# A fused mixture-of-experts layer with fp32 split products: up sum and h of both tiles in PSUM, and a new order of products and copies

## The reference

```python
g = jnp.einsum('bsd,edf->ebsf', h, Wg)
u = jnp.einsum('bsd,edf->ebsf', h, Wu)
expert_outs = jnp.einsum('ebsf,efd->ebsd', jax.nn.silu(g) * u, Wd)
expert_output = jnp.einsum('be,ebsd->bsd', gating_probs, expert_outs)
shared = jnp.einsum('bsf,fd->bsd', jax.nn.silu(h @ Sg) * (h @ Su), Sd)
out = x + (1.0 - sg) * expert_output + sg * shared
```

## Time and profile before

| what | value |
|---|---|
| median of 3 runs | 2305.16 us (2304.65 to 2307.76) |
| profiled execution | 2306.76 us |
| its span, first to last instruction | 2305.0 us |
| mean granted TensorE clock | 0.998 of full speed |
| TensorE busy | 2246.9 us (97%), 9504 matmuls |
| DVE, POOL, ACT busy | 78%, 72%, 62% |
| HBM traffic | 53 GB/s over the span |

### The profile page before, as it was taken

How to read it: one execution, slowest core, us unless ns; L and a number is a source line. 1 busy time by engine, 2 the same in 40 slices (tenths; PEclk the granted TensorE clock), 3 DMA queues, 4 the chain that set the end, 5 groups by cost and what they waited for, 6 DMA issues and landing times.

```text
span 2305.0 us, 33781 instructions
## 1 busy us (share of the span) xinstructions
PE 2246.9 (97%) x9504; PEld 1765.6 (77%) x9504; DVE 1802.1 (78%) x2622; ACT 1430.8 (62%) x2334; POOL 1651.5 (72%) x2055
## 2 busy tenths in 40 slices
PE   6999999999999999999999999999999999999998
PEld 4777777777777777777777777777777777777776
DVE  6777777777777777777777777777778778777787
ACT  5666666666666666666666666666666666666664
POOL 7877777777887767767787677677676677677663
PEclk9999999999999999999999999999999999999999
DMA  4111111111111111111121111111112111111110
GB/s 136 55 48 55 48 48 55 48 48 55 60 56 48 52 51 48 51 51 48 50 64 56 48 48 55 48 48 55 48 48 67 55 48 48 54 48 49 54 48 25
DMA packets 44170, 122.21 MB, mean 53 GB/s; under 512 B 4928, under 2 KB 4944, under 8 KB 44128
## 3 DMA queue, kind: packets, MB, share of 16 engines
q1 hardware_dynamic: 44064, 121.65, 17.1%
q0 software_dynamic: 64, 0.07, 0.1%
HBM read 117.51 MB, written 4.19 MB: 53 GB/s over the span
## 4 chain that ended last, share of the span: by engine, by line
PE 49%; DVE 25%; issue 16%; ACT 8%; DVEq 1%; ACTq 1%; DMA 0%; SPq 0%; POOL 0%
DVE h L422 16%; PE chain_ps L256 9%; DVE up L450 8%; ACT tap_p L353 7%; PE chain_ps L258 6%; PE down_ps L256 6%; PE down_ps L258 6%; PE chain_ps L257 6%; PE down_ps L257 6%; PE p_ps L256 3%; PE p_ps L257 3%; PE p_ps L258 3%; DVEq L118 0%; ACTq L118 0%; DMA acc<-xT 0%
## 5 line engine op out<-in xcount | busy, mean ns | idle before, releaser
L183 POOL TENSOR_TENSOR w_lo<-w_raw,w_hi 128x384 fp32r<-128x384 f32 x864 | 912.1, 1085 | 593.9 <-ACT w_hi L323 593.8
L345 ACT CAST h_hi<-h 128x512 fp32r<-128x512 f32 x576 | 361.4, 627 | 658.1 <-DVE h L422 653.1
L168 POOL TENSOR_TENSOR w_raw<-w_raw 128x128 f32<-128x128 f32 x1152 | 700.6, 628 | 33.6 <-DMA acc<-xT 8.8
L422 DVE SCALAR_TENSOR_TENSOR h<-silu,coef,up 128x256 f32<-128x256 f32 x576 | 607.6, 1093 | 32.7 <-DVE up L450 7.5
L256 PE MATMUL chain_ps<-x_hi,w_hi 128*128 128x512 f32 x1152 | 480.0, 417 | 44.1 <-POOL w_lo L183 20.1
L444 DVE TENSOR_TENSOR gate<-tap_u,p_ps 128x512 f32<-128x512 f32 x288 | 198.0, 687 | 397.6 <-PE p_ps L258 397.6
L256 PE MATMUL down_ps<-h_hi,w_hi 128*128 128x512 f32 x1152 | 452.0, 392 | 8.3 <-DVE h_lo L430 8.3
L257 PE MATMUL chain_ps<-x_lo,w_hi 128*128 128x512 f32 x1152 | 450.6, 391 | 0.0
L258 PE MATMUL chain_ps<-x_hi,w_lo 128*128 128x512 f32 x1152 | 450.6, 391 | 0.0
L258 PE MATMUL down_ps<-h_hi,w_lo 128*128 128x512 f32 x1152 | 449.8, 390 | 0.0
L257 PE MATMUL down_ps<-h_lo,w_hi 128*128 128x512 f32 x1152 | 449.2, 390 | 0.0
(11 more groups left out here) (38 smaller groups left out, 2125.8 us busy)
## 6 DMA issues: line engine op xcount, KB each, us to landing
w_raw<-w SPq DMA_DIRECT2D x288, 384.0 KB, 3.0
outT<-acc SPq DMA_DIRECT2D x8, 512.0 KB, 4.7
acc<-xT SPq DMA_DIRECT2D x6, 512.0 KB, 9.2
acc<-xT SPq DMA_DIRECT2D x4, 256.0 KB, 6.2
probs_sb<-probs POOLq DMA_DIRECT2D x1, 64.0 KB, 5.3
shared_sb<-shared_gate POOLq DMA_DIRECT2D x1, 8.0 KB, 6.5
```

Source lines behind the costliest of these rows:

```text
L168: nc.gpsimd.tensor_tensor(raw[:, cols(dst, dst)], raw[:, cols(a, a)], raw[:, cols(b, b)], op).then_inc(w_sums, 1)
L183: ins = nc.gpsimd.tensor_tensor(w_lo[:, s, c], w_raw[:, s, c], w_hi[:, s, c].bitcast(F32), ALU.subtract)
L345: nc.scalar.copy(h_hi[:, t], h[:, t]).then_inc(h_hi_done[t], 1)
L422: ins = nc.vector.scalar_tensor_tensor(h[:, 1, s], silu[:, 1, s], coef_of(g, e, 1, half), up1[:, s], ALU.mult, ALU.mult)
```

## The change

1. `up1` and `h` leave SBUF. The up sum of tile 1 is written by DVE into the bank in which p2 was (`p2_up1_ps`), h of tile 1 over it, and h of tile 0 over its own chain bank. The hi and lo parts of tile 0's h have two buffers, those of tile 1 one.
2. TensorE's order in chunk n becomes: p4 of chunk n-1, p1, p5, down of tile 0 of chunk n-2, p6, p2, p3, p7, down of tile 1 of chunk n-1. p1 waits for h_lo of tile 0 of chunk n-2, which reads its bank; p2 for h_lo of tile 1 of chunk n-1.
3. ACT's order: h_hi of tile 1 (n-1), tap_p1, tap_p5, h_hi of tile 0 (n-1), weight_hi part 0 (six forms, A11 to D1) of chunk n+2, tap_u2, weight_hi part 1 (S1, S2, S4), token copies, silu 0, silu 1.
4. DVE's order: h_lo of tile 1 (n-1), h of tile 0 (n-1), h_lo of tile 0 (n-1), gate 0, gate 1, up1, h of tile 1. The adds of a group stand one in the first and one in the second chunk of the next.
5. POOL's wait for the next group's tokens moves to where it forms T1.

The diff, cut to its core:

```diff
-        p2_ps = ctx.enter_context(nc.psum_tensor("p2_ps", [P, TOKENS], F32))
+        p2_up1_ps = ctx.enter_context(nc.psum_tensor("p2_up1_ps", [P, TOKENS], F32))
...
                 if form == T1:
+                    pool.wait_ge(pair_loaded[g - 1], 32)
...
-                if g + 1 < GROUPS:
-                    pool.wait_ge(pair_loaded[g], 32)
...
+                if not isinstance(n, int) or n > 0:
+                    p4(g - 1 if first else g, (k - 1) % CHUNKS, n - 1, first=in_first and k == 1)
 
                 pe.wait_ge(w_lo_done, n + 1)
-                after(pe, h0_done, n - 1)
-                product(chain, s, A11, *x(B11), start=True, stop=True).then_inc(p1_done, 1)
+                after(pe, h_lo_done[0], n - 1)
+                product(chain, s, A11, *x_of(g, B11, first), start=True, stop=True).then_inc(p1_done, 1)
                 after(pe, gate1_done, n)
-                product(p53_ps[:], s, S1, *x(T1), start=True, stop=True).then_inc(p5_done, 1)
-                after(pe, gate0_done, n)
-                product(p2_ps[:], s, A12, *x(B21), start=True, stop=True).then_inc(p2_done, 1)
+                product(p53_ps[:], s, S1, *x_of(g, T1, first), start=True, stop=True).then_inc(p5_done, 1)
+                if not isinstance(n, int) or n > 1:
+                    pe.wait_ge(h_lo_done[0], n - 1)
...
+                    down0((k - 2) % CHUNKS, start=opens, stop=in_first and k == 1)
                 pe.wait_ge(p1_tapped, n + 1)
...
+                after(pe, h_lo_done[1], n)
+                product(p2_up1_ps[:], s, A12, *x_of(g, B21, first), start=True, stop=True).then_inc(p2_done, 1)
...
-            def weight_hi(n, s):
+            def weight_hi(n, s, part):
+
                 act.wait_ge(w_sums, 4 * (n + 1))
                 after(act, down_done[0], n - SLOTS + 1)
-                nc.scalar.copy(w_hi[:, s, :], w_raw[:, s, :]).then_inc(w_hi_done, 1)
+                c = slice(0, S1 * P) if part == 0 else slice(S1 * P, FORMS * P)
+                nc.scalar.copy(w_hi[:, s, c], w_raw[:, s, c]).then_inc(w_hi_done, 1)
...
                 if not first:
-                    h_hi_of(0, n - 1, h0_done)
+                    h0_hi_of(n - 1, k - 1)
+                if ahead:
+                    weight_hi(n + AHEAD, (k + AHEAD) % SLOTS, 0)
                 act.wait_ge(p6_done, n + 1)
                 after(act, gate1_done, n)
                 nc.scalar.copy(tap_u2[:], chain_ps[:, k % 2, :]).then_inc(u2_tapped, 1)
...
                     ins = nc.vector.scalar_tensor_tensor(
-                        h[:, 1, s], silu[:, 1, s], coef_of(g, e, 1, half), up1[:, s], ALU.mult, ALU.mult
+                        p2_up1_ps[:, s], silu[:, 1, s], coef_of(g, e, 1, half), p2_up1_ps[:, s], ALU.mult, ALU.mult
                     )
...
-                after(dve, h1_done, n)
-                nc.vector.tensor_tensor(up1[:], tap_p5[:], chain_ps[:, k % 2, :], ALU.add).then_inc(up1_done, 1)
+                dve.wait_ge(gate0_done, n + 1)
+                nc.vector.tensor_tensor(p2_up1_ps[:], tap_p5[:], chain_ps[:, k % 2, :], ALU.add).then_inc(up1_done, 1)
...
-                if closes and before[0] >= 0:
-                    for t in (1, 0):
-                        add(before[0], t, n - 1)
+                if isinstance(e, int) and e == 0 and g > 0:
+                    if k == 0:
+                        add(g - 1, 1, n - 1)
+                    if k == 1:
+                        add(g - 1, 0, n - 2)
```

More of the change, by code:

```diff
@@ L57, in moe_kernel @@
         gate = sb("gate", [P, 2, TOKENS])
-        up1 = sb("up1", [P, TOKENS])
         silu = sb("silu", [P, 2, TOKENS])
-        h = sb("h", [P, 2, TOKENS])
-        h_hi = sb("h_hi", [P, 2, TOKENS], F32R)
-        h_lo = sb("h_lo", [P, 2, TOKENS], F32R)
+        h0_hi = sb("h0_hi", [P, 2, TOKENS], F32R)
+        h0_lo = sb("h0_lo", [P, 2, TOKENS], F32R)
+        h1_hi = sb("h1_hi", [P, TOKENS], F32R)
+        h1_lo = sb("h1_lo", [P, TOKENS], F32R)
         probs_sb = sb("probs_sb", [P, BATCH, ROUTED])
@@ L258, in product, with x_of, down0, down1 @@
                 return nc.tensor.matmul(bank, w_lo[:, s, c], hi, start=False, stop=stop, **on)
-            def down(g, k, t, start, stop):
+            def x_of(g, form, first):
+                if first:
+                    pe.wait_ge(x_lo_done, X_FORMS * g + form + 1)
+                return x_hi[:, g % 2, form, :], x_lo[:, g % 2, form, :]
+            def down0(k, start, stop):
                 for c in range(DC):
                     last = product(
-                        down_ps[:, t, c, :], k % SLOTS, D0 + c, h_hi[:, t, :], h_lo[:, t, :], start, stop
+                        down_ps[:, 0, c, :], k % SLOTS, D0 + c, h0_hi[:, k % 2, :], h0_lo[:, k % 2, :], start, stop
                     )
-                last.then_inc(down_done[t], 1)
-            def unit(g, e, k, first=False):
+                last.then_inc(down_done[0], 1)
+            def down1(k, start, stop):
+                for c in range(DC):
+                    last = product(down_ps[:, 1, c, :], k % SLOTS, D0 + c, h1_hi[:], h1_lo[:], start, stop)
+                last.then_inc(down_done[1], 1)
+            def p4(g, k, n, first=False):
+                pe.wait_ge(up1_done, n + 1)
+                x = x_of(g, T4, first)
+                product(chain_ps[:, k % 2, :], k % SLOTS, A22, *x, start=False, stop=True, goes_on=True).then_inc(
+                    p4_done, 1
+                )
+            def unit(g, e, k):
                 n = g * PER + e * CHUNKS + k
@@ L271, in unit @@
                 chain = chain_ps[:, k % 2, :]
[L273 to L280, removed]
+                in_first = isinstance(e, int) and e == 0
@@ new lines, in unit @@
+                if not isinstance(n, int) or n > 1:
+                    pe.wait_ge(h_lo_done[0], n - 1)
+                    opens = in_first and k == 2
+                    if opens:
+                        after(pe, added[0], g)
+                    down0((k - 2) % CHUNKS, start=opens, stop=in_first and k == 1)
+                pe.wait_ge(p1_tapped, n + 1)
+                product(chain, s, S2, *x_of(g, T2, first), start=False, stop=True, goes_on=True).then_inc(p6_done, 1)
+                after(pe, h_lo_done[1], n)
@@ L291, in unit @@
+                product(p2_up1_ps[:], s, A12, *x_of(g, B21, first), start=True, stop=True).then_inc(p2_done, 1)
+                pe.wait_ge(p5_tapped, n + 1)
+                product(p53_ps[:], s, S4, *x_of(g, B22, first), start=False, stop=True, goes_on=True).then_inc(p3_done, 1)
+                pe.wait_ge(u2_tapped, n + 1)
+                product(chain, s, S3, *x_of(g, T3, first), start=False, stop=True, goes_on=True).then_inc(p7_done, 1)
                 if not isinstance(n, int) or n > 0:
@@ L292, in unit @@
                     pe.wait_ge(h_lo_done[1], n)
[L293 to L306, removed]
+                    opens = in_first and k == 1
+                    if opens:
+                        after(pe, added[1], g)
@@ L308, in _ @@
+                    down1((k - 1) % CHUNKS, start=opens, stop=first)
             for g in range(GROUPS):
                 for k in range(CHUNKS):
-                    unit(g, 0, k, first=(k == 0))
+                    unit(g, 0, k)
                 with pe.Fori(1, EXPERTS) as e:
@@ L339, in x_form_hi, with h1_hi_of, h0_hi_of @@
                 nc.scalar.copy(x_hi[:, g % 2, form], full).then_inc(x_hi_done, 1)
[L341 to L345, removed]
+            def h1_hi_of(n):
+                act.wait_ge(h1_done, n + 1)
+                after(act, down_done[1], n)
+                nc.scalar.copy(h1_hi[:], p2_up1_ps[:]).then_inc(h_hi_done[1], 1)
+            def h0_hi_of(n, k):
+                act.wait_ge(h0_done, n + 1)
+                after(act, down_done[0], n - 1)
+                nc.scalar.copy(h0_hi[:, k % 2], chain_ps[:, k % 2, :]).then_inc(h_hi_done[0], 1)
             def unit(g, e, k, new_x=False):
@@ L349, in unit @@
                 first = isinstance(n, int) and n == 0
+                ahead = not isinstance(n, int) or n + AHEAD <= LAST
+                if not first:
+                    h1_hi_of(n - 1)
                 act.wait_ge(p1_done, n + 1)
@@ L361, in unit @@
                 nc.scalar.copy(tap_u2[:], chain_ps[:, k % 2, :]).then_inc(u2_tapped, 1)
+                if ahead:
+                    weight_hi(n + AHEAD, (k + AHEAD) % SLOTS, 1)
+                if new_x:
+                    for form in X_AT.get(k, ()):
+                        x_form_hi(g + 1, form)
                 act.wait_ge(gate0_done, n + 1)
@@ L437, in gate0 @@
                 after(dve, silu_done[0], n)
[L438 removed]
+                nc.vector.tensor_tensor(gate[:, 0], tap_p1[:], p2_up1_ps[:], ALU.add).then_inc(gate0_done, 1)
             def gate1(n):
```

61 lines of the change are left out of this document (32 added, 29 removed).

## The result

The changed kernel takes 2184.81 us (median of 4 runs, 2184.52 to 2185.44). The kernel before took 2306.46 us beside it (4 runs), a ratio of 0.9473 with a 95% interval of 0.9457 to 0.9490. The forecast was 2181 us, with 2173 to 2224 as the range.

What follows compares the result with a forecast made beforehand. TensorE's matmuls and their waits for tap_p1 bound the kernel; without waits, 288 x 7.48 = 2154.2 us, plus first matmul at 15.7, start and tail waits 2.8, 1.3, 0.8, and end 5.8, gives 2180.6, median 2181; range 2173 to 2224.

Steps and rivals of the forecast that it cites:

- 282 x 0.38: Crosscheck of the steady chunks: 282 waits for tap_p1, 0.38 us each, come to 107 us gained.
- What moves is S2, which gets the down products of tile 0 in front of it: ACT order: tap_p1 is released at 2.19 us of the chunk, S2 stands at 3.40, 1.2 us of slack.
- the ring: Chain of waits from S3 through up1, h1, its copies, w_hi part 0 and tap_u2 to the next S3.
- The second rival: New h1 stays slow at 2.14 us a pair, S3 0.76 late per chunk: 2400 us, chance 0.04.
- The ring's slack of 0.5 us: Across a chunk: tap_u2 released at 12.41 us, next S3 due at 12.92, slack 0.5 us.
- The margin of 0.37 at tap_u2: Split w_hi copy: tap_u2, behind part 0, is ready at 5.07 us, S3 needs it at 5.44.
- The group change: Token group change: one add in each of two chunks starts h1_lo 0.5 us later, within the slack; no cost taken.
- The start: POOL's moved token wait: weight slot 1 lands at 10.9, first matmul at 15.7 us, 4.4 us earlier.
- The slow matmuls at the start, 2.8 in the sum: First 13 matmuls take 5.71 us instead of 2.95, as in the kernel before; 2.8 us added.
- 4.9: Extra TensorE time: slow first matmuls 2.8, first A22's wait for up1 1.3, last down's wait for h_lo 0.8 us.
- 5.8: End of the span: 6.1 us from the last matmul's start to the end, less one slot of 0.23.
- the last step of the sum: From span to median: profiled execution 1.76 us above its span, median 1.6 below that, so 2181 us.

Runs made afterwards that it cites:

- up sum alone: Kernel before with only the up sum of tile 1 moved to PSUM, into p2's bank; order, h in SBUF and the two adds stay: 2191.51 us, ratio 0.9503.
- order only: Changed kernel with the up sum of tile 1 back in SBUF, h's result still in PSUM, new order kept: 2319.65 us, ratio 1.0060 to the kernel before.
- the whole copy: Changed kernel with w_hi copied in one piece of 1152 columns ahead of tap_u2 instead of in two parts: 2192.80 us.
- The run with the wait put back: Changed kernel with POOL's wait for the next tokens back at the head of each group: 2187.47 us.
- the start with the first w_lo first: Changed kernel with POOL forming the first chunk's w_lo ahead of the second chunk's weight sums: 2186.00 us.

## Why the prediction was right

**The bound.** Right, and as worked out: without a wait the period is 7.48 us, in every chunk but the first ones and the last. (This is TensorE's own pace of 33 matmuls.) The earlier trace rows had it already; the gain in the steady part, 282 x 0.38, could be read from the kernel before alone.

**h1.** Right in cause and size: 0.88 us. The rule of the Trainium skill on two SBUF inputs ("SBUF — State Buffer", "Who interferes with whom") is borne out twice, each time in one schedule: 1093 against 479 ns a half in the old order (kernel before, up sum alone), 1063 against 487 in the new one (order only, changed kernel). That it needs POOL's reads, as the rule says, and not its writes, no run separates. The rule of the Trainium skill, "VectorE: DVE Perf Modes", section "The TRN2 errata", that a PSUM source costs 0.065 us more does not show at that size: h_lo from PSUM takes 692 ns, and DVE's token rests, subtractions of the same size with both sources in SBUF, take 685 while POOL is idle. The prediction compared 0.69 with h_lo's 0.71, which holds waits for POOL as well.

**What the order does.** Here the prediction gave credit where little was due. "What moves is S2, which gets the down products of tile 0 in front of it" is true, but tap_p1's wait goes in the old order too, as soon as h1 is short. The new order is worth at most about 2 us, and without the short h1 it makes the kernel slower than before, because it puts the weight copy and tap_u2 behind the ring that h1 delays.

**The margins.** The second rival put a slow h1 at 2400 us, and the order-only run gives 2319.65. The ring's slack of 0.5 us was the term that was too small: ACT's instructions start about 0.1 us before the one ahead ends, which the sum left out. With 1.2 us more in h1 and 0.47 of it lost, restart of 0.1 included, the slack was about 0.8. The margin of 0.37 at tap_u2, on the other hand, left out the weight load, which wants to start 0.23 us earlier; the whole copy shows it. Both rest on one thing, that a row's start and end are not the limits of when the neighbour can go.

**The group change.** Right: one add moved h_lo by 0.4 us (564.72 instead of 564.34, a period after 556.86), and nothing waits.

**The start.** Wrong by 2.5 us: 18.22 instead of 15.7. Slot 1 landed as forecast (10.73 against 10.9). The step that failed is taking POOL's 1.85 and 2.92 us from rows where DVE was at its coefficients. Moved 4.5 us earlier, POOL's sums and rests meet DVE's token rests, which read two SBUF tensors each, and they hold each other up: POOL 7.5 us instead of 4.8, DVE 0.94 to 1.49 an instruction instead of 0.69. It was the same contention that I had named for h1, and I didn't ask whom the moved step would meet. The run with the wait put back shows it: there DVE is done with the rests as POOL starts, and both have their old times. The slow matmuls at the start, 2.8 in the sum, were fewer: the first 7 distances took 3.15 us, 1.6 more than 7 slots. That took half of it back, and it was luck, since other runs with the same start had up to twice as many.

**Sum.** Forecast of the span: 15.7 + 2154.2 + 4.9 + 5.8 = 2180.6, in other words 15.7 to the first matmul, 2158.9 to the start of the last, 6.1 to the end (one slot moves from the second part to the third). Measured: 18.2, 2158.5 and 6.0, together 2182.7. So the span explains 2.1 of the 3.8 us between 2181 and 2184.81. The rest is the last step of the sum: it took the median to be 1.6 us below the profiled execution, as in the kernel before, and here it is 0.3 above it (2184.52).

## What to carry to other kernels

When an instruction that should be short shows a duration that is close to that of another engine's instruction beside it (h1 1093 ns, w_lo 1085), look in the same trace for a stretch in which the other is idle: it gives both the cause and the period that is left without it. Where a tensor lies can be worth far more than the order (here 115 us against 2); try the one edit before rebuilding the schedule, since a denser schedule makes the same slow instruction costlier. And a step that is moved earlier keeps its duration only if its new neighbours don't hold it up as h1 was held up.

## What the runs showed of the hardware

POOL gains nearly as much as DVE: its weight sums fell from 628 to 465 ns a piece, w_lo from 1085 to 1018, without an edit there. The short h1 alone took the sums to 586 (up sum in PSUM alone); the rest of the change, in which h_lo reads PSUM too and the order is another, took them to 465. TensorE's period did not need this gain. A DVE instruction that reads and overwrites one PSUM bank (h1, 487 ns a half) is as fast as one that reads PSUM and writes SBUF (479). After a stall of 0.89 us (group change, up sum in PSUM alone) the matmuls went on 0.23 us apart. After 2.6 us (the same place before) and after 2.5 and 3.2 us (the start with the first w_lo first) some were 0.43 apart; the profile shows a granted clock of 0.51 from 603.0 to 606.4 of the kernel before, and of 0.50 from 24.6 to 30.0 of the other run.
